# Four of sixteen states' du times B made in a turned layout by ScalarE and TensorE, and half of the projection down moved to the routing stage

## The reference, cut to what matters

```python
delta = softplus(dt_proj_w @ dt_lo + dt_proj_b)          # (b, 1024 channels, 1024 rows)
A = -exp(A_log)                                          # 16 states
def step(state, xs):
    d_t, B_t, C_t, u_t = xs
    dA = exp(d_t[..., None] * A)
    state = state * dA + (d_t * u_t)[..., None] * B_t[:, None, :]
    y_t = einsum('ben,bn->be', state, C_t)
    return (state, y_t)
...
y = (y + D[None, :, None] * u) * silu(z)                 # z: layernorm(x)
x = x + tanh(g_xattn) * swapaxes(y, 1, 2)
...
_, idx = top_k(scores, k)                                # 128 rows of each sequence
mlp = silu(h2 @ w_gate) * (h2 @ w_up) @ w_down           # on the chosen rows
```

## Time and profile before

| | us |
|---|---|
| median of 3 runs (lowest to highest) | 3016.49 (3014.51 to 3021.93) |
| profiled execution, own time | 3018.8 |
| its span in the trace | 3017.1 |
| scan 0, first scan to last gate | 184.3 to 1024.1 |
| scan 1, first scan to last gate | 1417.9 to 2298.0 |
| routing 1 | 2307.7 to 2392.2 |

### The profile page before, as it was taken

One profiled execution on the slowest core, in us unless ns is written; L12 is line 12 of the kernel. 1 busy time (PEld: TensorE's weight loads), 2 busy tenths in 40 slices (PEclk: granted clock), 3 DMA queues, 4 the chain that ended last, 5 costly groups with the idle time before them and its releaser, 6 DMA issues. The chain is left out here.

```text
span 3017.1 us, 30047 instructions
## 1 busy us (share of the span) xinstructions
PE 2392.6 (79%) x10552; PEld 1599.2 (53%) x10552; DVE 2110.9 (70%) x2626; ACT 1338.0 (44%) x2470; POOL 1683.2 (56%) x600
## 2 busy tenths in 40 slices
PE   7857777778777547986888888888883299999998
PEld 3334444444444326653767666654552186668863
DVE  4569999999999674432999999999997633310000
ACT  3457755566655342242665555665552212410000
POOL 1169999999999401003998898999993100000000
PEclk9969999989999758998999999999997599999999
DMA  7722252342522396745236335336333543144543
GB/s 259 253 90 75 67 158 77 113 139 63 164 66 60 115 374 208 287 134 189 84 105 197 99 104 186 109 98 216 98 108 133 204 170 98 50 144 151 152 153 104
DMA packets 224869, 426.70 MB, mean 141 GB/s; under 512 B 17488, under 2 KB 101712, under 8 KB 221904
## 3 DMA queue, kind: packets, MB, share of 16 engines
q1 hardware_dynamic: 211216, 368.68, 38.3%
q10 hardware_dynamic: 12160, 51.39, 4.3%
q0 software_dynamic: 1344, 4.72, 0.4%
HBM read 340.84 MB, written 83.89 MB: 141 GB/s over the span
## 5 line engine op out<-in xcount | busy, mean ns | idle before, releaser
L600 POOL TENSOR_TENSOR s_x<-s_du,k_bB 128x2048 f32<-128x2048 f32 x256 | 1156.3, 4533 | 80.8 <-PE s_py L663 52.0
L896 ACT ACTIVATE s_pA<-s_delta,k_negA 128x512 f32<-128x512 f32 x1024 | 664.1, 680 | 382.7 <-DVE s_x L947 373.9
L663 PE MATMUL s_py<-k_ident,s_x 128*128 128x128 f32 x4096 | 582.8, 289 | 260.6 <-DVE s_x L947 253.2
L663 PEld LDWEIGHTS s_py<-k_ident,s_x 128*128 128x128 f32 x4096 | 506.8, 150 | 489.3 <-DVE s_x L947 347.2
L962 DVE TENSOR_TENSOR_SCAN s_pA<-s_pA,s_x 128x512 f32<-128x512 f32 x384 | 452.2, 1214 | 40.9 <-POOL s_x L600 38.3
L947 DVE TENSOR_TENSOR s_x<-s_pA,k_bC 128x1024 f32<-128x1024 f32 x384 | 464.2, 1209 | 19.1 <-DMA k_bC<-scratch_xd 19.0
L962 DVE TENSOR_TENSOR_SCAN s_pA<-s_pA,s_carry,s_x 128x512 f32<-128x512 f32 x384 | 472.6, 1275 | 2.0 <-POOL s_x L600 1.6
L1570 PE MATMUL l_p<-l_hT,l_ring 128*128 128x256 f32 x1792 | 397.0, 381 | 2.5 <-DVE l_hT L1784 1.4
L1570 PEld LDWEIGHTS l_p<-l_hT,l_ring 128*128 128x128 f32 x1792 | 341.9, 191 | 50.2 <-issue 2.0
L607 POOL TENSOR_TENSOR s_x<-s_hp,k_bC 128x1024 f32<-128x1024 f32 x128 | 302.2, 2361 | 15.8 <-DVE s_hp L962 15.5
L1577 PE MATMUL l_p<-l_ring,l_hidden 128*128 128x512 f32 x512 | 220.9, 592 | 1.7 <-DMA l_ring<-in_wo 1.7
(11 more groups left out here) (200 smaller groups left out, 3100.1 us busy)
## 6 DMA issues: line engine op xcount, KB each, us to landing
k_bB<-scratch_xd SPq DMA_DIRECT2D x32, 1024.0 KB, 11.8
k_bC<-scratch_xd SPq DMA_DIRECT2D x32, 1024.0 KB, 12.3
scratch_ug<-p_ug ACTq DMA_DIRECT2D x16, 1024.0 KB, 4.0
k_u<-scratch_ug SPq DMA_DIRECT2D x64, 256.0 KB, 3.6
s_gy<-scratch_ug SPq DMA_DIRECT2D x64, 256.0 KB, 4.2
s_xt<-in_x SPq DMA_DIRECT2D x64, 256.0 KB, 4.6
...
```

The costliest lines, as they stand in the source:

```text
L600: pool.tensor_tensor(out=x[:, 4 * g:4 * g + 4], in0=du[:, s % 2:s % 2 + 1].broadcast_to([P, 4, HALF]), in1=bB[:, 4 * g:4 * g + 4], op=ALU. ...
L663: last = nc.tensor.matmul(py[:, a], x[:, n, a * P:(a + 1) * P], ident[:], is_transpose=True, start=False, stop=is_last and a == HALF // P - 1)
L896: nc.scalar.activation(pA[:, n % 4], delta[:, s % 2], ACT.Exp, scale=negA[:, s % NE, n:n + 1]).then_inc(dA_ready, 1)
```

## The change

Of pairs 3 and 7 (states 6, 7, 14, 15; `TURNED`), du times B no longer comes from GpSimd. TensorE turns du into `pm` (`turn_du`), ScalarE copies it to `duT` with rows as partitions (`copy_du`) and multiplies it by B, there one number for each partition, in four pieces of 128x128 for each state (`make_state`, sixteen pieces a unit), and TensorE turns the products into `pA` (`turn_x`). The dA of these pairs goes to SBUF (`x`) instead, so the two inputs of the scan trade places. `BT`, B with rows on partitions, is loaded by DMAs of single 4-byte elements, four a chunk. Groups 1 and 3 of `quad` shrink to two states. GpSimd takes three pairs times C (1, 3, 5) instead of two, so VectorE has five instead of six. `add_x` moves from TensorE, `pm` and a ScalarE copy to one GpSimd addition. Slots are set anew. The chunk's other loads keep their order.

Of the projection down, one half of the 1024 output columns stays in scan 1; the other goes to routing 1: 64 matmuls of 128x512 on TensorE, 32 of them ahead of `spread(0)` and 32 ahead of `spread(1)`, with 16 loads of 512 KB on SP and two copies by ScalarE at the end. `hidden` is kept over the stages (`Through`), and other tiles share its space.

```diff
-        self.bB = sb("bB", [P, NS, HALF])
+        self.bB = sb("bB", [P, NS - 4, HALF])
...
+        self.BT = sb("BT", [P, 2, 4, HALF // P])
...
+    def load_columns(self, sp, t, b, th, j, sem):
+        for k, n in enumerate((6, 7, 14, 15)):
+            at = b * ND + NR + n
+            sp.dma_start(self.BT[:, j, k], t["xd"][at:at + 1, th * HALF:(th + 1) * HALF].rearrange("n (a p) -> p (n a)", p=P),
+                         allow_slow_non_contiguous=True).then_inc(sem, 16)
...
-POOL_PAIRS = (2, 5)
+POOL_PAIRS = (1, 3, 5)
+TURNED = (3, 7)
 VEC_PAIRS = tuple(i for i in range(NPAIR) if i not in POOL_PAIRS)
-SUM_ORDER = (0, 1, 3, 2, 4, 6, 5, 7)
+SUM_ORDER = (0, 1, 2, 4, 3, 5, 6, 7)
+NT = 2 * len(TURNED)
...
-GATE_AT, TURN_AT, DT_AT = 2, 3, 6
-READ_AT, X2_AT, COPY_AT = 2, 5, 7
+GATE_AT, TURN_AT, DU_AT, DT_AT = 2, 0, 2, 5
+READ_AT, COPY_AT, DU_COPY_AT = 1, 5, 6
+STATE_AT = (6, 7, 4, 5)
...
-FILL = (2, 2, 3, 3, 3, 3, 4, 5)
+FILL = (1, 3, 7, 1, 1, 2, 3, 3)
...
-DOWN_FROM = (GATE_UP + 10, GATE_UP + 16 + DOWN_HALF)
-FILL_END = DOWN_FROM[1] + DOWN_HALF
-SIZE_LAG, LOG_LAG, SIGMOID_LAG, SWISH_LAG, MERGE_LAG, COPY_LAG = 4, 4, 7, 6, 4, 3
+DOWN_FROM = GATE_UP + 10
...
+                if c >= 2:
+                    sp.wait_ge(xT_ready, NT * NE * (c - 1))
+                keep.load_columns(sp, t, b, th, c % 2, BT_in[c % 2])
...
+                pairs = tuple(i for i in (2 * g, 2 * g + 1) if i not in TURNED)
+                many = 2 * len(pairs)
...
-                    pool.wait_ge(summed, max(after_sum(s - 1, 2 * g), after_sum(s - 1, 2 * g + 1)))
-                pool.tensor_tensor(out=x[:, 4 * g:4 * g + 4], in0=du[:, s % 2:s % 2 + 1].broadcast_to([P, 4, HALF]),
-                                   in1=bB[:, 4 * g:4 * g + 4], op=ALU.mult).then_inc(w_ready, 1)
+                    pool.wait_ge(summed, max(after_sum(s - 1, i) for i in pairs))
+                pool.tensor_tensor(out=x[:, 4 * g:4 * g + many], in0=du[:, s % 2:s % 2 + 1].broadcast_to([P, many, HALF]),
+                                   in1=bB[:, 3 * g + g % 2:3 * g + g % 2 + many], op=ALU.mult).then_inc(w_ready, 1)
...
+            def add_x(s):
+                pool.wait_ge(y_used, s + 1)
+                pool.wait_ge(xt_in[s % 3], ring3(s)[1])
+                pool.tensor_tensor(out=xt[:, s % 3], in0=xt[:, s % 3], in1=gy[:, s % 3], op=ALU.add).then_inc(x2_ready, 1)
...
             for s in range(UNITS):
                 quad(s, 2)
                 quad(s, 3)
-                times_C(s, 2)
+                times_C(s, 1)
                 if s + 1 < UNITS:
                     begin(s + 1)
                 quad(s + 1, 0)
+                times_C(s, 3)
                 times_C(s, 5)
                 quad(s + 1, 1)
+                if s:
+                    add_x(s - 1)
+            add_x(UNITS - 1)
 
...
-                if s == 1:
-                    pe.wait_ge(dt_read, 1)
-                if s >= 2:
-                    pe.wait_ge(gate_turned, s - 1)
+                if s:
+                    pe.wait_ge(duT_ready, s)
...
+                pe.wait_ge(dt_read, min(s + 2, UNITS))
...
+            def turn_du(s):
+                pe.wait_ge(du_ready, s + 1)
+                if s:
+                    pe.wait_ge(gate_turned, s)
+                for a in range(HALF // P):
+                    last = nc.tensor.transpose(pm[:, a * P:(a + 1) * P], du[:, s % 2, a * P:(a + 1) * P], ident[:])
+                last.then_inc(du_turned, 1)
+
+            def turn_x(s, i):
+                pe.wait_ge(scanned, NS * s + 2 * i - 2)
+                for n in (2 * i, 2 * i + 1):
+                    k = state_at(0, n) - 1
+                    pe.wait_ge(xT_ready, state_at(s, n))
+                    for a in range(HALF // P):
+                        last = nc.tensor.transpose(pA[:, n % 4, a * P:(a + 1) * P], xT[:, k, a * P:(a + 1) * P], ident[:])
+                    last.then_inc(x_turned, 1)
 
...
+            turn_du(0)
             dt_proj(1)
             for s in range(UNITS):
+                turn_x(s, TURNED[0])
                 if s >= 2:
                     pe.wait_ge(u_in[s % 2], 16 * (s // 2))
...
+                    if i == TURNED[1] - 3:
+                        turn_x(s, TURNED[1])
                     if at == TURN_AT:
                         turn_gate(s)
+                    if at == DU_AT and s + 1 < UNITS:
+                        turn_du(s + 1)
...
+            def copy_du(s):
+                act.wait_ge(du_turned, s + 1)
+                act.wait_ge(xT_ready, NT * s)
+                nc.scalar.activation(duT[:], pm[:], ACT.Copy).then_inc(duT_ready, 1)
+
+            def make_state(s, k):
+                if s >= UNITS:
+                    return
+                if k == 0:
+                    act.wait_ge(duT_ready, s + 1)
+                    if s and s % NE == 0:
+                        act.wait_ge(BT_in[chunk(s) % 2], 64 * ((chunk(s) + 1) // 2))
+                if s:
+                    act.wait_ge(x_turned, NT * (s - 1) + k + 1)
+                for a in range(HALF // P):
+                    last = nc.scalar.activation(xT[:, k, a * P:(a + 1) * P], duT[:, a * P:(a + 1) * P], ACT.Copy,
+                                                scale=BT[:, chunk(s) % 2, k, a:a + 1])
+                last.then_inc(xT_ready, 1)
 
...
+                    if i in TURNED and s:
+                        act.wait_ge(summed, after_sum(s - 1, i))
                     for n in (2 * i, 2 * i + 1):
-                        nc.scalar.activation(pA[:, n % 4], delta[:, s % 2], ACT.Exp, scale=negA[:, s % NE, n:n + 1]).then_inc(dA_ready, 1)
+                        out = x[:, n] if i in TURNED else pA[:, n % 4]
+                        nc.scalar.activation(out, delta[:, s % 2], ACT.Exp, scale=negA[:, s % NE, n:n + 1]).then_inc(dA_ready, 1)
...
-                    if i == X2_AT and s:
-                        copy_x2(s - 1)
                     if i == COPY_AT:
                         copy_gate(s)
+                    if i == DU_COPY_AT and s + 1 < UNITS:
+                        copy_du(s + 1)
+                    for k in range(NT):
+                        if i == STATE_AT[k]:
+                            make_state(s + (k < 2), k)
...
+                dA, added = pA[:, n % 4], x[:, n]
+                if i in TURNED:
+                    dve.wait_ge(x_turned, state_at(s, n))
+                    dA, added = added, dA
+                nc.vector.tensor_tensor_scan(out, dA, added, initial, ALU.mult, ALU.add).then_inc(scanned, 1)
...
+            def load_weights(j):
+                if j >= RING:
+                    sp.wait_ge(w_used, j - RING + 1)
+                sp.dma_start(ring[:, j % RING].rearrange("p (a c) -> p a c", c=HALF),
+                             t["w_down"][2 * j * P:(2 * j + 2) * P, HALF:].rearrange("(a p) c -> p a c", p=P)).then_inc(w_in[j % RING], 16)
...
+                if not late and k % 2 and k // 2 <= RING:
+                    load_weights(k // 2 - 1)
...
+            def feed_forward(begin, end):
+                for m in range(begin, end):
+                    if m % 2 == 0:
+                        pe.wait_ge(w_in[m // 2 % RING], 16 * (m // 2 // RING) + 16)
+                    for a in range(SPAN):
+                        last = nc.tensor.matmul(p_down[a][:], keep.hidden[:, m, a * P:(a + 1) * P],
+                                                ring[:, m // 2 % RING, m % 2 * HALF:(m % 2 + 1) * HALF], start=m == 0, stop=m == NI - 1)
+                    if m % 2:
...
+            else:
+                feed_forward(0, NI // 2)
...
+            else:
+                feed_forward(NI // 2, NI)
```

More of the change, by code:

```diff
@@ L349, in scan_stage @@
     act_chain, u_scaled = sem("act_chain"), sem("u_scaled")
+    du_turned, duT_ready, xT_ready, x_turned = (sem(n) for n in ("du_turned", "duT_ready", "xT_ready", "x_turned"))
+    BT_in = [sem(f"BT_in{j}") for j in range(2)]
     dt_in = [sem(f"dt_in{j}") for j in range(2)]
@@ L701, in feed_forward @@
                         gate_up(k)
-                    for h in range(H2):
-                        at = k - DOWN_FROM[h]
-                        if 0 <= at < DOWN_HALF and at % 2 == 0:
-                            down(h, at // (2 * SPAN), at // 2 % SPAN)
+                    at = k - DOWN_FROM
+                    if 0 <= at < DOWN_HALF and at % 2 == 0:
+                        down(at // (2 * SPAN), at // 2 % SPAN)
             def late_projection(s, i):
@@ L738, in _ @@
                     pe.wait_ge(y_used, s)
-                    add_x(s - 1)
                 skip(s)
@@ L760, in _ @@
                     late_convolution(UNITS - 1, i)
-            add_x(UNITS - 1)
             if fill:
@@ L890, in _ @@
                 act.wait_ge(act_chain, 2)
+            copy_du(0)
+            make_state(0, 0)
+            make_state(0, 1)
             for s in range(UNITS):
@@ L1102, in _ @@
                     load_pre(k)
+            if not late:
+                for j in range(RING, NI // 2):
+                    load_weights(j)
```

(9 more changed lines are left out.)

133 lines of the change are left out of this document (66 added, 67 removed).

## The result

The changed kernel takes 3023.3 us (median of 20 runs), the kernel before in the same session 3014.9: a ratio of 1.0024, with 95% interval 1.0015 to 1.0033. So it is slower by a quarter of a per cent, where 2998 and "faster" were forecast. The profiled executions have spans of 3021.9 and 3017.1 us.

| | before | after | difference | forecast |
|---|---|---|---|---|
| scan 0 | 839.8 | 828.1 | -11.7 | -19 |
| scan 1 | 880.1 | 884.2 | +4.1 | -13 |
| ends of both scans | 22.4 | 17.8 | -4.7 | -2 |
| routing 1 | 84.5 | 102.4 | +17.9 | +16 |
| all other stages | | | within 0.5 each | 0 |

What follows compares the result with a forecast made beforehand. VectorE's list was taken to bound both scans. The terms -36.2 x 2 + 22 x 2 + 5 - 9 - 3 + 1 + 16 = -18 us gave 2998 against the median of 3016.5; range of 8 in 10: 2948 to 3034.

Steps and rivals of the forecast that it cites:

- Change 1: In both scans VectorE loses one states times C of six a unit: 36.2 us less in each scan.
- Change 3: In the scans ScalarE gets the turned states, so VectorE waits for it: +22 us a scan, +5 more in scan 1.
- the ladder: ScalarE's step-by-step path from pair 2's times C to state 14's scan; lateness averages 0.70 us a unit, +22 a scan.
- Rival 1: ScalarE keeps up in the scans, since stalls elsewhere give slack: 49 us come back, 2949 us; chance 0.20.
- Change 4: TensorE's work and order in the scans cost 0 beside ScalarE's stall; granted clock stays above 0.9.
- The +5 given to ScalarE's steps there: In scan 1 ScalarE's feed-forward steps fall into the slots of about half the 16 pieces: +5 us, bounds -5 and +15.
- Change 5: Loads of C at a chunk's first unit come earlier, halving VectorE's 19.0 us of waits: -9 us, bounds -19 and +10.
- Changes 2, 6, 7: GpSimd's list in the scans, 0; ends of the scans, -3 and +1; 64 more matmuls in routing 1, +16 us.
- rival 2: Routing 1 runs its matmuls at 1.2 GHz: +63 us there instead of +16, 3045 us in all; chance 0.11.
- rival 4: TensorE's clock falls to 0.50 in scan 0, 20 us a unit becoming 38: +400 us; chance 0.02.
- by GpSimd: Rival: GpSimd becomes the scans' bound at 26.4 us a unit, +1.0 x 32 in scan 0, 3031 us; chance 0.12.

## Why the prediction was wrong

- **Change 1** (-36.2 a scan): its 64 operations are gone (x320 instead of x384), but VectorE's busy time fell by 30.0 in scan 0. The durations of its instructions add up to 37.4 us less, but the time by which neighbours overlap also shrank, from 64.5 to 57.0 us: a scan that comes late, be it by too little for the list of waits, loses its 0.1 us of overlap. In the unit of the timeline state 10 starts 2.41 us after state 8 (249.03 - 246.62) instead of 2 x 1.12, so it is 0.17 late, where the forecast had 0.25 (0.16 in the mean of first halves).
- **Change 3** (+22 a scan): right in scan 0. 15.9 us of listed waits for state 14 and those 6 stand for it. The place was right, and so was the sum, but the chain was too long: slots 4 and 5, which the ladder counted in, have slack, as two experiments showed. Rival 1 (ScalarE keeps up) is wrong in the kernel as it is, and moving 1.2 us by one slot brings nearly half of the 49 us that it would have given, 14 of them in scan 0.
- **Change 4** (0, "it costs 0.1 to 0.5 a unit in scan 1 if ScalarE's is smaller"): **this step failed.** The path was followed and came out at 9.7, equal to ScalarE's, and was then priced at nothing. It came out equal only with every step on time and every matmul at full clock ("seven feed-forward matmuls of 0.43", 3.0 us). With 0.3 us to spare in the first unit shown, each lateness of the gate's copy or of TensorE's own start came through to VectorE; and while TensorE waited for that copy, its granted clock fell to 0.50 (1.2 GHz) in 12 of 31 units, which made the way from du's turning to state 14's some 1.7 us longer, up to 2.5 us of wait in a unit. As an estimate from the lengths of these stretches, 13 to 14 of the 17.6 us of waits come of the slower clock; no run changed the clock alone. The order was worth 22 us in scan 1 (30 without the steps). The +5 given to ScalarE's steps there don't explain that scan 1 got slower: leaving them out gained 20.7 in the changed kernel and 30.5 in the one before.
- **Change 5** (-9): failed as well, with less weight; it is most of what scan 0 missed. Groups 2 and 3 went as forecast. That a load stands behind the store, and that the store now waits for GpSimd's last step (`add_x`), was not followed through SP's queue; it ate 10 us, which the loads' new order gave back.
- **Changes 2, 6, 7** (0, -2, +16): right in the main. GpSimd was no bound (773 and 775 us busy, VectorE hardly ever waited for it), the ends gave 4.7, and routing 1 cost 17.9 (its first rank slipped by 12.3 where 9 were forecast).
- **The clock** (rivals 2 and 4): in the mean granted 0.92 and 0.93 in the scans as before (0.92, 0.94), with 20 transposes more a unit, so rival 4 did not come. But "stays above 0.9" is true of the mean alone: under change 4 it is 0.50 just where VectorE waits for TensorE. In routing 1 it was 0.80, where it was 0.50 (1.2 GHz) with 12.7 us of work, so rival 2 did not come either. The rule of the Trainium skill (TensorE: Matmul & The Clock Gate, Part 4) that transposes are not clock work is neither borne out nor refuted: scan 0 kept its projection and convolution matmuls, and nothing here ran on transposes alone.

By stages the time is 24 us over the forecast: 17 in scan 1, 7 in scan 0, 2 in routing 1, less 3 at the ends. The run with only `FILL` changed takes 2999.9 us, 2 from the forecast. That is in part luck: its scan 0 is still short of the forecast, and its scan 1 and the ends are above it. Slower had been given a chance of 0.21, by routing 1 at 1.2 GHz and by GpSimd, and neither was the cause.
